# The expert stage of a two-layer transformer block: gathered rows turned by transposing DMAs instead of by TensorE

## The chip, the cores and the metric

The kernel runs on one core of a Trainium2 chip. The metric is the device time of one execution in microseconds; the median over the runs is quoted. A profile of one execution gives every instruction of the engines: TensorE (PE, and PEld for its weight loads), VectorE (DVE), ScalarE (ACT), GpSimd (POOL), SyncE (SP, which here only issues DMAs and waits).

## The reference

Two layers run over x of 16 x 100 tokens by 512. Only the end of the second layer, a mixture of 32 experts, is touched by the change:

```python
logits = x @ gate_weight.T                     # 1600 tokens, 32 experts
topv, topi = top_k(softmax(logits), 8)         # then scaled, cut at TAU, renormalised -> combine
def expert_step(acc, xs):
    w_gu, w_d, c_e = xs
    gu = x @ w_gu.T                            # 512 -> 2 x 192
    g, u = split(gu, 2)
    h = silu(g) * u
    acc = acc + h @ w_d.T * c_e[:, None]       # 192 -> 512
```

The result is added to x. Before it come an attention with latent keys, a feed-forward layer with ternary weights and a second, causal attention, each on a layer norm of x.

## The kernel before

Only the rows that an expert is really chosen for are computed. The stage `route` sorts the (token, expert) pairs into 131 tiles of up to 128 rows, each tile of one expert, and writes the row numbers to `core.sources`. The normed rows lie in HBM in `xtab`: for each token 512 columns of 4 bytes, which hold 1024 half-precision numbers (the 512 numbers as a high and a low half), and behind them 32 weights, one per expert.

The stage `experts` then goes through the tiles. The engines run their own programs, and semaphores order them:

- POOL (line 2686 on) gathers tile i + 8 by an indirect DMA into one of NX = 8 slots of `xg`, and scatters the finished rows of a tile with an add into one of NACC = 2 sums in HBM (`acc`). Scatter i waits for scatter i - 2 to have landed, and a gather into a slot waits until that slot's rows were turned.
- TensorE (line 2714 on) turns the gathered rows (`turn_x`): eight transposes of 128 x 128 into the bank `x_ps`, since the contraction must lie along the partitions. `up` makes 12 matmuls with 384 columns into `g_ps` (high and low halves of both operands, without low times low), `turn_h` turns h by three transposes into `h_ps`, and `downs` makes five matmuls with 512 columns into `d_ps`.
- VectorE copies `x_ps` to `xT` (`copy_x`, two buffers), multiplies (`product`), and makes the low half of h (`low`).
- ScalarE applies the silu (`silu`), makes the high half of h (`high`), copies `h_ps` to `hT` (`copy_h`) and scales the finished rows by the expert's weight (`weigh`).
- SP loads the weights of the next experts into a ring of four (line 2345 on), once the tiles of an older expert are done.

TensorE's order in the step of tile i is: `downs(i - 2)`, `turn_x(i + 1)`, the first half of `up(i)`, `turn_h(i - 1)`, the second half of `up(i)`. ScalarE's is: `weigh(i - 2)`, `copy_h(i - 1)`, `silu(i)`, `high(i)`. VectorE's is: `copy_x(i + 1)`, `product(i)`, `low(i)`. At the end the two sums in HBM are loaded, added and stored.

Of the kernel before, what the change touches and what calls it, by code (L numbers as in the profile page):

```python
# [19 lines left out]
ACT = mybir.ActivationFunctionType  # L20
# [5 lines left out]
P = 128  # L26
# [2299 lines left out]
TABLE = -(-TILES // GROUP) * GROUP  # L2326
FAR = 32768.0
ROUND = 1.5 * 2.0 ** 23
NX, NACC, NO = 8, 2, 6


class ExpertWeights:
# [289 lines left out]
def experts(core, t, ew, out):  # L2622

    nc = core.nc
    x_in = Slots(core, "slots_in", NX, per=16)
    x_turned, x_copied = Steps(core, "x2_turned"), Steps(core, "x2_copied")
    gu, gated, made = Steps(core, "gu2_sum"), Steps(core, "silu2"), Steps(core, "h2")
    h_hi, h_lo = Steps(core, "h2_hi"), Steps(core, "h2_lo")
    h_turned, h_copied = Steps(core, "h2_turned"), Steps(core, "h2_copied")
# [5 lines left out]
    back, summed, stored = Slots(core, "acc_back", PARTS, per=16 * NACC), core.sem("acc_summed"), core.sem("stored")  # L2635
    with ExitStack() as ctx:
        xg = core.xg
        xT = core.sb(ctx, "xT", [P, 2, 2 * KT, P], F16)
        sg = core.sb(ctx, "sg2", [P, 2, INTER], F32)
        hf = core.sb(ctx, "hf2", [P, 2, INTER], F32)  # L2640
        hc = core.sb(ctx, "hc2", [P, 2, 2, INTER], F16)
# [1 line left out]
        rows = core.sb(ctx, "rows2", [P, NO, DIM], F32)  # L2643
        total = [core.accT[:, :, :].rearrange("p k n -> p (k n)")]
        total += [core.sb(ctx, f"end_rows{k}", [P, FLAT], F32) for k in range(1, NACC)]
        x_ps = core.banks(ctx, "x2_ps", 2, F32)
        g_ps = core.banks(ctx, "g2_ps", 2)
        h_ps = core.banks(ctx, "h2_ps", 2, F32)
        d_ps = core.banks(ctx, "d2_ps", 2)
# [1 line left out]
        def half(bank, n):  # L2651
            return bank[:, 0:n * P // 2].bitcast(F16).rearrange("p (k s) -> p k s", k=n)
# [7 lines left out]
        with nc.Block() as block:  # L2660
# [24 lines left out]
            @block.gpsimd  # L2685
            def _(pool):
                def gather(i):
                    if i >= NX:
                        pool.wait_ge(x_turned.sem, x_turned.after(i - NX))
                    nc.gpsimd.indirect_dma_start(  # L2690
                        out=xg[:, i % NX, :], out_offset=None, in_=core.xtab[:, :],
                        in_offset=bass.IndirectOffsetOnAxis(ap=core.sources[:, i:i + 1], axis=0),
                        bounds_check=TOK - 1, oob_is_err=False).then_inc(x_in[i % NX].sem, 16)

                def scatter(i):
                    pool.wait_ge(weighed.sem, weighed.after(i))
                    if i >= NACC:
                        o = i - NACC
                        pool.wait_ge(put[o % NO].sem, put[o % NO].after(o // NO))
                    nc.gpsimd.indirect_dma_start(  # L2700
                        out=core.acc[i % NACC][:, :],
                        out_offset=bass.IndirectOffsetOnAxis(ap=core.sources[:, i:i + 1], axis=0),
                        in_=rows[:, i % NO, :], in_offset=None, bounds_check=TOK - 1, oob_is_err=False,
                        compute_op=ALU.add).then_inc(put[i % NO].sem, 16)

                for i in range(NX):
                    gather(i)
                for i in range(TILES):
                    scatter(i)
                    if i + NX < TILES:  # L2710
                        gather(i + NX)

            @block.tensor
            def _(pe):
                place = {}

                def turn_x(i):
                    pe.wait_ge(x_in[i % NX].sem, x_in[i % NX].after(i // NX))
                    if i >= 2:
                        pe.wait_ge(x_copied.sem, x_copied.after(i - 2))  # L2720
                    parts = xg[:, i % NX, 0:DIM].bitcast(F16)
                    for k in range(2 * KT):
                        last = nc.tensor.transpose(half(x_ps[i % 2], 2 * KT)[:, k, :], parts[:, k * P:(k + 1) * P],  # L2723
                                                   core.ident_h[:, :])
                    last.then_inc(x_turned.sem, 1)

                def ring(i, col, n, parts=P):
                    return ew.ring[0:parts, bass.ds(place[i][0] + col, n)]

# [13 lines left out]

                def up(i, terms):
                    if terms[0] == TERMS[0]:
                        pe.wait_ge(x_copied.sem, x_copied.after(i))
                        if i >= 2:
                            pe.wait_ge(made.sem, made.after(i - 2))
                        pe.wait_ge(w_ready, place[i][1])
                    for k, w, a in terms:  # L2750
                        last = nc.tensor.matmul(g_ps[i % 2][:, 0:2 * INTER], xT[:, i % 2, a * KT + k, :],  # L2751
                                                ring(i, (2 * k + w) * 2 * INTER, 2 * INTER),
                                                start=((k, w, a) == TERMS[0]), stop=((k, w, a) == TERMS[-1]))
                    if terms[-1] == TERMS[-1]:
                        last.then_inc(gu.sem, 1)
# [20 lines left out]

                load_place(0)
                check_place(0)
                turn_x(0)
                for i in range(TILES + 2):  # L2780
                    if i >= 2:
                        downs(i - 2)
                    if i + 1 < TILES:
                        turn_x(i + 1)
                    if i < TILES:
                        up(i, TERMS[0:6])
                    if 1 <= i < TILES + 1:
                        turn_h(i - 1)
                    if i < TILES:
                        up(i, TERMS[6:9])  # L2790
                    if i + 1 < TILES:
                        if (i + 1) % GROUP == 0:
                            load_place(i + 1)
                        check_place(i + 1)
                    if i < TILES:
                        up(i, TERMS[9:12])

            @block.scalar
            def _(act):
                col = {}  # L2800

                def silu(i):
                    act.wait_ge(gu.sem, gu.after(i))
                    if i >= 2:
                        act.wait_ge(made.sem, made.after(i - 2))
                    nc.scalar.activation(sg[:, i % 2, :], g_ps[i % 2][:, 0:INTER], ACT.Silu, scale=1.0 / W2  # L2806
                                         ).then_inc(gated.sem, 1)

                def high(i):
                    act.wait_ge(made.sem, made.after(i))  # L2810
                    if i >= 2:
                        act.wait_ge(h_turned.sem, h_turned.after(i - 2))
                    nc.scalar.activation(hc[:, i % 2, 0, :], hf[:, i % 2, :], ACT.Copy).then_inc(h_hi.sem, 1)  # L2813

                def copy_h(i):
                    act.wait_ge(h_turned.sem, h_turned.after(i))
                    if i >= 2:
                        act.wait_ge(down.sem, down.after(i - 2))
                    nc.scalar.activation(hT[:, i % 2], half(h_ps[i % 2], 3), ACT.Copy).then_inc(h_copied.sem, 1)  # L2819

                def weigh(i):
                    if i % GROUP == 0:
                        _, regs = nc.values_load_multi_w_load_instructions(
                            core.tile_tab[0:1, i // GROUP, 2, :], engines=[mybir.EngineType.Activation],
                            min_val=0, max_val=DIM + NEXP - 1,
                            skip_runtime_bounds_check_because="made from an expert's number, at most NEXP - 1")
                        for g in range(GROUP):
                            col[i + g] = regs[g]
                    act.wait_ge(down.sem, down.after(i))
                    if i >= NO:  # L2830
                        act.wait_ge(put[i % NO].sem, put[i % NO].after(i // NO - 1))
                    scale = xg[:, i % NX, bass.ds(col[i], 1)]
                    nc.scalar.activation(rows[:, i % NO, :], d_ps[i % 2][:, :], ACT.Copy, scale=scale  # L2833
                                         ).then_inc(weighed.sem, 1)

                for i in range(TILES + 2):
                    if i >= 2:
                        weigh(i - 2)
                    if 1 <= i < TILES + 1:
                        copy_h(i - 1)  # L2840
                    if i < TILES:
                        silu(i)
                        high(i)

            @block.vector
            def _(dve):
                def copy_x(i):
                    dve.wait_ge(x_turned.sem, x_turned.after(i))
                    if i >= 2:
                        dve.wait_ge(gu.sem, gu.after(i - 2))  # L2850
                    nc.vector.tensor_copy(xT[:, i % 2], half(x_ps[i % 2], 2 * KT)).then_inc(x_copied.sem, 1)  # L2851

                def product(i):
                    dve.wait_ge(gated.sem, gated.after(i))
# [8 lines left out]
                    nc.vector.tensor_tensor(hc[:, i % 2, 1, :], hf[:, i % 2, :], hc[:, i % 2, 0, :], ALU.subtract  # L2863
                                            ).then_inc(h_lo.sem, 1)

                copy_x(0)
                for i in range(TILES):
                    if i + 1 < TILES:
                        copy_x(i + 1)
                    product(i)  # L2870
                    low(i)
                for k in range(PARTS):
                    dve.wait_ge(back[k].sem, back[k].after(0))
                    nc.vector.tensor_tensor(total[0][:, piece(k)], total[0][:, piece(k)], total[1][:, piece(k)],  # L2874
# [110 lines left out]
```

## Time and profile before

| what | value |
|---|---|
| time, three runs | 1844.2, 1845.92, 1846.16 us; median 1845.92 |
| span of the profiled execution, first to last instruction | 1842.9 us |
| busy in the span: PE, DVE, ACT, POOL | 87%, 65%, 56%, 33% |
| mean granted TensorE clock over the span | 0.931 |
| expert stage: first gather, last `d_ps` group, last scatter begin at | 1323.81, 1812.15, 1814.98 us |

The profile states no time of its own for its execution beside the span; the median of the runs is 3.0 us above the span. In the profile an instruction stands with its engine, its line, and the tiles that it writes and reads (`out<-in`). A granted clock of 1.00 means 2.4 GHz, 0.50 means 1.2 GHz. The DMA share is the mean busy share of the core's 16 DMA engines. q1 is the queue of DMAs that SP issues, q10 that of ScalarE's, q0 that of POOL's.

### The profile page before, as it was taken

How to read it: one execution, taken by the hardware profiler on the slowest of the kernel's cores; microseconds unless marked ns; L12 is line 12 of the kernel's file. 1: busy time of each engine (PE TensorE's matmuls, PEld its weight loads, DVE VectorE, ACT ScalarE, POOL GpSimd, SP SyncE). 2: the span in 40 equal slices, each digit the busy share in tenths (PEclk: the TensorE clock that was granted, in tenths of full speed). 3: DMA queues.
4: the chain of work that ended last, by engine and by line, in shares of the span. 5: the costliest groups of instructions: out<-in, count | busy, mean ns of one | idle time of the engine just before them, and what ended most of it. 6: DMA issues, size and time to landing. Idle time of an engine off the chain costs nothing. (4 is left out here: it accounts for less than half of the span.)

```text
span 1842.9 us, 35610 instructions
## 1 busy us (share of the span) xinstructions
PE 1606.8 (87%) x11911; PEld 998.5 (54%) x11911; DVE 1192.0 (65%) x2678; ACT 1036.1 (56%) x2563; POOL 611.1 (33%) x481
## 2 busy tenths in 40 slices
PE   4788999999999979989997777784599999999993
PEld 3655656656656545555554454553466666666661
DVE  4866797787787779688796777757633333333332
ACT  3447746746747627566574777743655555455451
POOL 4614304304304300000000222212167777777662
PEclk9789999999999989999998998776599999999996
DMA  8820120220120249787786001104356656556536
GB/s 271 285 84 9 55 75 9 62 68 10 65 65 10 69 157 333 239 280 241 227 260 227 12 2 37 36 29 114 78 108 140 150 136 140 137 129 136 131 74 225
DMA packets 143332, 226.57 MB, mean 123 GB/s; under 512 B 37857, under 2 KB 93409, under 8 KB 143032
## 3 DMA queue, kind: packets, MB, share of 16 engines
q1 hardware_dynamic: 107160, 195.90, 33.6%
q0 software_dynamic: 29344, 21.29, 7.1%
q10 hardware_dynamic: 6656, 7.11, 1.1%
q8 instruction: 105, 1.72, 0.4%
q14 instruction: 67, 0.55, 0.1%
HBM read 175.00 MB, written 98.80 MB: 149 GB/s over the span
## 5 line engine op out<-in xcount | busy, mean ns | idle before, releaser
L2751 PE MATMUL g_ps<-ring,xT 128*128 x1572 | 300.8, 327 | 1.1 <-issue 1.1
L1051 POOL TENSOR_TENSOR pr<-pr,sm 128x1444 f32<-128x1444 f32 (+1 forms) x64 | 137.3, 2145 | 385.9 <-DVE sm L1087 385.9
L2700 POOL DMA_INDIRECT acc<-rows,slot_sources x131 | 207.8, 1586 | 107.2 <-issue 78.7
L2857 DVE SCALAR_TENSOR_TENSOR hf<-sg,g_ps 128x192 f32<-128x192 f32 x131 | 46.4, 354 | 238.5 <-ACT sg L2806 206.3
L2751 PEld LDWEIGHTS g_ps<-ring,xT 128*128 128x128 f16 x1572 | 142.8, 98 | 71.9 <-issue 5.5
L2690 POOL DMA_INDIRECT xg<-xtab,slot_sources x131 | 138.0, 1054 | 81.3 <-issue 79.5
L2773 PE MATMUL d_ps<-ring,hT 128*128 x655 | 162.8, 379 | 1.6 <-ACT hT L2819 1.1
L1081 DVE TENSOR_REDUCE sm<-s_banks 128x2 f32<-128x722 f32 (+2 forms) x128 | 97.5, 762 | 67.3 <-PE s_banks L819 64.8
L973 ACT ACTIVATE pr<-s_banks,sm 128x361 f32<-128x361 f32 (+1 forms) x208 | 115.3, 563 | 30.7 <-DVE sm L1081 29.2
L876 PE MATMUL o_bank<-cT,N_hi 128*128 128x400 f16 x512 | 129.7, 335 | 0.0
L819 PE MATMUL s_banks<-kvp,qp 128*128 128x361 f16 (+1 forms) x624 | 116.9, 318 | 10.8 <-ACT pr L973 6.1
L2098 POOL MEMSET zero_row<- 128x544 f32 x1 | 0.6, 557 | 377.5 <-POOLq L1338 377.5
L2819 ACT ACTIVATE hT<-h_ps 128x384 f16<-128x384 f16 x131 | 64.3, 491 | 101.8 <-PE h_ps L2764 99.3
L849 PE MATMUL o_bank<-probsT,kvp 128*128 128x384 f16 (+5 forms) x576 | 108.2, 333 | 1.1 <-DVE probsT L1092 1.1
L1230 ACT ACTIVATE split_o<-split_f 128x512 f16<-128x512 f32 (+1 forms) x192 | 87.9, 513 | 20.6 <-DMA split_f<-in_down 12.1
L2773 PEld LDWEIGHTS d_ps<-ring,hT 128*128 128x128 f16 x655 | 63.7, 97 | 65.6 <-issue 3.4
L2102 POOL TENSOR_TENSOR pr<-pr,sm 100x1600 f32<-100x1600 f32 x16 | 45.8, 2864 | 157.5 <-DVE sm L2173 157.5
L2833 ACT ACTIVATE rows<-d_ps,xg 128x512 f32<-128x512 f32 x131 | 90.0, 687 | 13.4 <-issue 2.2
L2851 DVE COPY xT<-x_ps 128x1024 f16<-128x1024 f16 x131 | 90.6, 692 | 10.1 <-issue 6.2
L1376 PE MATMUL gate_ps<-hT_hi,wt 128*128 128x400 f16 x256 | 86.8, 339 | 11.0 <-DVE hf L1506 9.2
L1396 PE MATMUL down_ps<-hid,wt 128*128 128x400 f16 x512 | 94.5, 345 | 0.7 <-DVE hid L1511 0.7
L2723 PEld LDWEIGHTS x_ps<-ident_h,xg 128*128 128x128 f16 x1048 | 70.0, 99 | 37.5 <-DMA xg<-xtab,slot_sources 7.1
(322 smaller groups left out, 3848.1 us busy)
## 6 DMA issues: line engine op xcount, KB each, us to landing
split_f<-in_gu SPq DMA_DIRECT2D x64, 384.0 KB, 4.5
split_gu<-split_o SPq DMA_DIRECT2D x64, 384.0 KB, 3.1
ring<-split_gu SPq DMA_DIRECT2D x32, 768.0 KB
head<-in_head SPq DMA_DIRECT2D x16, 864.0 KB
tern_w<-in_tern SPq DMA_DIRECT2D x48, 256.0 KB
split_f<-in_down SPq DMA_DIRECT2D x32, 384.0 KB, 4.2
split_d<-split_o SPq DMA_DIRECT2D x32, 384.0 KB, 3.8
ring<-split_d SPq DMA_DIRECT2D x32, 256.0 KB
```

Source lines behind the costliest of these rows:

```text
L819: last = nc.tensor.matmul(sbank[0:n, i, 0:KEYS], qp[:, a, bi, at:at + n], kvp[:, bi % 2, k].rearrange("p j d -> p (j d)")[:, 0:KEYS], star ...
L849: last = nc.tensor.matmul(ob[1][:, 0:width(s)], kvp[0:KEYT[u], bi % 2, k, u, :], pT[s % 2][0:KEYT[u], a, u, 0:width(s)], start=(j == 0), s ...
L876: op = nc.tensor.matmul(ob[m % 2][:, 0:CH], w[:, h, f], cT[:, a, :, h * SEQ:(h + 1) * SEQ], start=(t == 0), stop=(t == len(terms) - 1))
L973: nc.scalar.activation(pr[0:n, s % 3, i, :], sbank[0:n, i, 0:KEYS], ACT.Exp, bias=small[0:n, s % 3, 0, i:i + 1], accum_out=small[0:n, s % ...
L1051: nc.gpsimd.tensor_tensor(pr[:, s % 3, 0:n], pr[:, s % 3, 0:n], small[:, s % 3, 2, 0:n].unsqueeze(2).to_broadcast([P, n, KEYS]), ALU.mult) ...
L1081: nc.vector.tensor_reduce(small[0:n, s % 3, 0, first:last], sbank[0:n, first:last, 0:KEYS], AX, ALU.max, negate=True).then_inc(peak.sem, 1)
L1396: last = nc.tensor.matmul(d_ps[m % 2][:, 0:CH], core.wt[:, 2 * KT * HT // 4 + k, m * P:(m + 1) * P], hh[:, a, k, :], start=(k == 0 and a = ...
L2690: nc.gpsimd.indirect_dma_start(out=xg[:, i % NX, :], out_offset=None, in_=core.xtab[:, :], in_offset=bass.IndirectOffsetOnAxis(ap=core.sou ...
L2700: nc.gpsimd.indirect_dma_start(out=core.acc[i % NACC][:, :], out_offset=bass.IndirectOffsetOnAxis(ap=core.sources[:, i:i + 1], axis=0), in ...
L2751: last = nc.tensor.matmul(g_ps[i % 2][:, 0:2 * INTER], xT[:, i % 2, a * KT + k, :], ring(i, (2 * k + w) * 2 * INTER, 2 * INTER), start=((k ...
L2773: last = nc.tensor.matmul(d_ps[i % 2][:, :], hT[0:parts, i % 2, pair, :], ring(i, D + col * DIM, DIM, parts), start=(n == 0), stop=(n == 4))
L2851: nc.vector.tensor_copy(xT[:, i % 2], half(x_ps[i % 2], 2 * KT)).then_inc(x_copied.sem, 1)
```

## The change

The eight transposes of TensorE and VectorE's copy of their result go. In their place ScalarE issues one transposing DMA a tile, from `xg` (128 rows of 1024 half-precision numbers) straight into `xT`, which has NT = 4 buffers with a semaphore each. It is issued three tiles ahead, between `weigh(i - 2)` and `silu(i)`; it waits until the gather has landed and until the matmuls that read the buffer before are done. TensorE's `up(i)` waits for that DMA, and so does POOL's gather into the slot. VectorE takes `copy_h` over from ScalarE. The two PSUM banks `x_ps` are no longer used.

```diff
-NX, NACC, NO = 8, 2, 6
+NX, NACC, NO, NT = 8, 2, 6, 4
...
-    x_turned, x_copied = Steps(core, "x2_turned"), Steps(core, "x2_copied")
+    x_turned = Slots(core, "x2_turned", NT, per=16)
...
-        xT = core.sb(ctx, "xT", [P, 2, 2 * KT, P], F16)
+        xT = core.sb(ctx, "xT", [P, NT, 2 * KT, P], F16)
...
                 def gather(i):
                     if i >= NX:
-                        pool.wait_ge(x_turned.sem, x_turned.after(i - NX))
+                        o = i - NX
+                        pool.wait_ge(x_turned[o % NT].sem, x_turned[o % NT].after(o // NT))
...
-                def turn_x(i):
-                    pe.wait_ge(x_in[i % NX].sem, x_in[i % NX].after(i // NX))
-                    if i >= 2:
-                        pe.wait_ge(x_copied.sem, x_copied.after(i - 2))
-                    parts = xg[:, i % NX, 0:DIM].bitcast(F16)
-                    for k in range(2 * KT):
-                        last = nc.tensor.transpose(half(x_ps[i % 2], 2 * KT)[:, k, :], parts[:, k * P:(k + 1) * P],
-                                                   core.ident_h[:, :])
-                    last.then_inc(x_turned.sem, 1)
...
                     if terms[0] == TERMS[0]:
-                        pe.wait_ge(x_copied.sem, x_copied.after(i))
+                        pe.wait_ge(x_turned[i % NT].sem, x_turned[i % NT].after(i // NT))
...
-                turn_x(0)
                 for i in range(TILES + 2):
                     if i >= 2:
                         downs(i - 2)
-                    if i + 1 < TILES:
-                        turn_x(i + 1)
...
-                def copy_h(i):
-                    act.wait_ge(h_turned.sem, h_turned.after(i))
-                    if i >= 2:
-                        act.wait_ge(down.sem, down.after(i - 2))
-                    nc.scalar.activation(hT[:, i % 2], half(h_ps[i % 2], 3), ACT.Copy).then_inc(h_copied.sem, 1)
+                def turn_x(i):
+                    act.wait_ge(x_in[i % NX].sem, x_in[i % NX].after(i // NX))
+                    if i >= NT:
+                        act.wait_ge(gu.sem, gu.after(i - NT))
+                    nc.scalar.dma_start_transpose(xT[:, i % NT], xg[:, i % NX, 0:DIM].bitcast(F16)
+                                                  ).then_inc(x_turned[i % NT].sem, 16)
...
+                for i in range(NT - 1):
+                    turn_x(i)
                 for i in range(TILES + 2):
                     if i >= 2:
                         weigh(i - 2)
-                    if 1 <= i < TILES + 1:
-                        copy_h(i - 1)
+                    if i + NT - 1 < TILES:
+                        turn_x(i + NT - 1)
                     if i < TILES:
                         silu(i)
                         high(i)
...
-                def copy_x(i):
-                    dve.wait_ge(x_turned.sem, x_turned.after(i))
+                def copy_h(i):
+                    dve.wait_ge(h_turned.sem, h_turned.after(i))
                     if i >= 2:
-                        dve.wait_ge(gu.sem, gu.after(i - 2))
-                    nc.vector.tensor_copy(xT[:, i % 2], half(x_ps[i % 2], 2 * KT)).then_inc(x_copied.sem, 1)
+                        dve.wait_ge(down.sem, down.after(i - 2))
+                    nc.vector.tensor_copy(hT[:, i % 2], half(h_ps[i % 2], 3)).then_inc(h_copied.sem, 1)
...
-                copy_x(0)
-                for i in range(TILES):
-                    if i + 1 < TILES:
-                        copy_x(i + 1)
-                    product(i)
-                    low(i)
+                for i in range(TILES + 1):
+                    if i >= 1:
+                        copy_h(i - 1)
+                    if i < TILES:
+                        product(i)
+                        low(i)
```

## Rows read from the trace of the kernel before

**Rows 1.** View by windows: us, busy us of each engine, PEclk, DMA share, GB/s.

```profile
1372.00:1422.00 50.00, 49.96 (x382) 30.87 (x380) 18.86 (x41) 25.16 (x55) 35.98 (x28) 1.00 0.62 135
...
1722.00:1772.00 50.00, 49.59 (x382) 30.78 (x381) 19.51 (x42) 25.72 (x55) 36.13 (x28) 1.00 0.51 120
```

**Rows 2.** The view by lines, 1350 to 1840 us, forms kept apart.

```profile
L2700 POOL DMA_INDIRECT acc<-rows,slot_sources x128 | 203.0, 1586 | 100.4 <-issue 78.4 <-ACT rows L2833 19.2 <-DMA acc<-rows,slot_sources 2.8
...
L2690 POOL DMA_INDIRECT xg<-xtab,slot_sources x121 | 127.5, 1054 | 36.9 <-issue 35.1 <-DMA acc<-rows,slot_sources 1.8
L2833 ACT ACTIVATE rows<-d_ps,xg 128x512 f32<-128x512 f32 x128 | 87.9, 687 | 13.0 <-issue 2.2 <-PE d_ps L2773 0.8
L2851 DVE COPY xT<-x_ps 128x1024 f16<-128x1024 f16 x125 | 86.5, 692 | 2.9 <-PE x_ps L2723 0.2
...
L2819 ACT ACTIVATE hT<-h_ps 128x384 f16<-128x384 f16 x127 | 62.4, 491 | 98.8 <-PE h_ps L2764 96.3 <-issue 2.4
```

**Rows 3.** The timeline of one tile, start us, us, engine.

```profile
1569.65 0.49 ACT L2819 ACTIVATE hT<-h_ps 128x384 f16<-128x384 f16 x1 [0.52 <-PE h_ps L2764]
...
1570.42 1.24 PE L2773 MATMUL d_ps<-ring,hT 128*128 x5
1570.62 0.33 ACT L2806 ACTIVATE sg<-g_ps 128x192 f32<-128x192 f32 x1 [0.48 <-PE g_ps L2751]
...
1571.77 0.36 DVE L2863 TENSOR_TENSOR hc<-hf,hc 128x192 f16<-128x192 f32 x1 [0.43 <-ACT hc L2813]
1571.88 0.69 ACT L2833 ACTIVATE rows<-d_ps,xg 128x512 f32<-128x512 f32 x1
...
1572.76 0.32 PEld L2764 LDWEIGHTS h_ps<-ident_h,hc 128*128 128x128 f16 x3
```

**Rows 4.** The timeline of TensorE, the last tiles.

```profile
1802.54 1.24 PE L2773 MATMUL d_ps<-ring,hT 128*128 x5
...
1806.18 1.24 PE L2773 MATMUL d_ps<-ring,hT 128*128 x5
...
1809.38 1.24 PE L2773 MATMUL d_ps<-ring,hT 128*128 x5
```

**Rows 5.** The timeline of POOL beside a load of weights.

```profile
1566.80 1.59 POOL L2700 DMA_INDIRECT acc<-rows,slot_sources  x1 [1.50 <-DMA acc<-rows,slot_sources]
1568.70 1.05 POOL L2690 DMA_INDIRECT xg<-xtab,slot_sources  x1 [0.30 <-issue]
1570.06 1.59 POOL L2700 DMA_INDIRECT acc<-rows,slot_sources  x1 [0.31 <-issue]
...
1573.37 1.59 POOL L2700 DMA_INDIRECT acc<-rows,slot_sources  x1 [0.32 <-issue]
```

**Rows 6.** DMA queues of 1350 to 1800, 16 to 114, 1815.5 to 1823 us: packets, MB, share.

```profile
q1 hardware_dynamic: 33152, 38.55, 30.1%
q0 software_dynamic: 27299, 19.18, 26.3%
...
q10 hardware_dynamic: 6656, 7.11, 21.1%
...
q1 hardware_dynamic: 463, 2.66, 93.5%
```

**Rows 7.** DMA issues: ns min/median/max of three lines, then one's landing in us.

```profile
L475 ACTq DMA_DIRECT2D lat_parts<-lat_parts_sb x16: 520/521/581, 18.1 to 111.6; - x16
...
L473 ACTq DMA_DIRECT2D kv_parts<-kv_parts_sb x16: 321/327/352, 17.7 to 111.2; - x16
...
L2352 SPq DMA_DIRECT2D ring<-split_d x32: 626/632/1705, 1277.6 to 1753.4; - x32
...
ternary<-tern_o SPq DMA_DIRECT2D x48, 128.0 KB, 1.7
```

**Rows 8.** The timeline of POOL and TensorE at the stage's start.

```profile
1323.81 1.28 POOL L2690 DMA_INDIRECT xg<-xtab,slot_sources  x1 [41.68 <-issue]
...
1327.61 1.04 PE L2723 MATMUL x_ps<-ident_h,xg 128*128 128x128 f16 x8 [6.06 <-DMA xg<-xtab,slot_sources]
```

More of the change, by code:

```diff
@@ L2645, in experts @@
         total += [core.sb(ctx, f"end_rows{k}", [P, FLAT], F32) for k in range(1, NACC)]
-        x_ps = core.banks(ctx, "x2_ps", 2, F32)
         g_ps = core.banks(ctx, "g2_ps", 2)
@@ L2750, in up @@
                     for k, w, a in terms:
-                        last = nc.tensor.matmul(g_ps[i % 2][:, 0:2 * INTER], xT[:, i % 2, a * KT + k, :],
+                        last = nc.tensor.matmul(g_ps[i % 2][:, 0:2 * INTER], xT[:, i % NT, a * KT + k, :],
                                                 ring(i, (2 * k + w) * 2 * INTER, 2 * INTER),
```

## The prediction

> **What bounds the kernel now.** I first read the windows of the expert stage, from the profile's start of the tile loop to its end, to see which engine has no gaps. Of eight windows of 50 us TensorE is busy 49.96 us in the first and 49.59 us in the last, at a granted clock of 1.00, which is the 2.4 GHz level [rows 1]. So the stage runs at TensorE's pace, and what is taken from TensorE there shortens the kernel until the next engine is full. The view by lines gives the price of each operation [rows 2], the timeline of one tile gives the order in which the engines hand work to each other [rows 3], and the timeline of the last tiles gives something rare: a tile of the same loop without the turning of x. From one start of the `d_ps` group to the next it is 3.64 us with the eight transposes (1802.54 to 1806.18) and 3.20 us without (1806.18 to 1809.38) [rows 4]. The timeline of POOL and the DMA views then give the two resources that are next [rows 5, 6].
>
> **What the change removes.** On TensorE: eight transposes a tile. By [rows 4] that is worth 3.64 - 3.20 = 0.44 us a tile, over 130 tile steps 57 us, and TensorE's own limit is then 3.20 us a tile. On VectorE: a copy of 692 ns a tile, replaced by the copy of h, 384 columns of 1024. Its price is between 692 x 384/1024 = 260 ns and ScalarE's 491 ns for the same tile [rows 2]. I take the middle, 0.38 us. ScalarE's copy now ends 0.28 us before the `d_ps` group that reads it (1570.14 against 1570.42) [rows 3], and VectorE's, which waits on the same `h_ps`, would not end later, so it costs nothing at either end. On ScalarE those 491 ns go. One cover gets thinner: the low half of h is ready at 1572.13, and TensorE loads it at 1572.76 [rows 3]; without the transposes ahead of it TensorE comes 0.44 us sooner, and 0.19 us are left. Whatever delays the silu by more than that is paid in full.
>
> **The scatter and gather engine is next.** POOL needs per tile 1.586 us for a scatter and 1.054 us for a gather [rows 2], with at least 0.31 and 0.30 us between them [rows 5]: 3.25 us, seen where it runs without waiting (1566.80 to 1570.06 in 3.26 us). It has 3.64 now. So of the 0.44 us at most 0.39 can be had: 3.25 us a tile instead of 3.20. The other thing POOL loses is its slack. Scatter number i waits for scatter i - 2 to land. At 1566.80 it waited 1.50 us instead of 0.31, during the transfer of an expert's weights [rows 5]; at 3.64 us a tile such a wait was made up in the next tiles, at 3.25 it is not. The ring holds four of the 32 experts at the start, so the stage loads 28, one in 131/28 = 4.7 tiles. If each cost this wait once, that were 1.19/4.7 = 0.25 us a tile; if none, 0. I take two of three, 0.17 us, because the time a scatter has to land falls by 2 x 0.39 = 0.78 us and the DMA engines get more to do. This gives 3.42 us a tile.
>
> **What the transposing DMA costs the DMA engines.** No row of before shows one. It moves 128 rows of 1024 half words, 256 KB. If a piece is one row of one block of 128 columns, 256 B, these are 1024 pieces, 64 for each of the 16 engines. The stage now uses 30.1 + 26.3 = 56.4% of the engines [rows 6], 2.05 us a tile. ScalarE's own queue moved 6656 packets in the first stage at 21.1% of 16 engines x 98 us, 49.7 ns for a mean of 1068 B; the large packets of the end took 93.5% x 16 x 7.5 us/463 = 242 ns for 5745 B, 42 ns for 1000 B [rows 6]. The first price is then 45 ns for bytes and 5 ns for the packet, and a piece of 256 B costs 11 + 5 = 16 ns: 64 pieces, 1.0 us. The weight loads in the stage cost 65 ns for 1163 B, 16 ns more than their bytes; by them a piece costs 27 ns, the transfer 1.7 us. At the full 49.7 ns it is 3.2 us. The bounds are 1.0 and 3.2 us. I take 1.0, since the row of ScalarE's queue is the nearest: same queue, SBUF as source, small pieces. The engines then have 3.05 us of work in 3.42, which is full but fits. Latency is covered: three transfers are ahead of the tile that is computed, 3 x 3.42 = 10 us, and a plain transfer of 128 KB lands in 1.7 us [rows 7].
>
> **What it costs ScalarE.** From the start of a silu to the end of the weighing after it 1.95 us pass (1570.62 to 1572.57) [rows 3]; then the new issue stands in ScalarE's queue, and behind it the next silu, for which VectorE's product, the turning of h and a later `d_ps` group wait. ScalarE's loop is thus 1.95 us + issue, and an issue up to 3.25 - 1.95 = 1.3 us is hidden by the TensorE work of the same tile; above that each microsecond lengthens each tile. Issues of plain DMAs on this queue took 327 ns (128 rows) and 521 ns (256 pieces), and one of SP's in the stage 632 ns, at worst 1705 ns [rows 7]. If the time grows by 194 ns for each further 128 pieces, 1024 pieces take 0.327 + 7 x 0.194 = 1.69 us. Bounds 0.33 and 1.69. I take 0.6, since SP's issue of several pieces a row does not grow so. The issue also waits for a gather three tiles ahead. The gather of tile j follows scatter j - 8. In tile step j - 6 the weighing ends 2.15 us after the `d_ps` group began, the scatter starts 0.80 us later (1572.57, 1573.37) [rows 3, 5], and with 1.59 + 0.30 + 1.05 us the gather is written out at 5.9 us. The first gather of the stage landed within 2.5 us after that (1325.09 to 1327.61) [rows 8], so it is there at 8.4 us, and ScalarE asks for it three steps later, at 3 x 3.25 + 2.15 = 11.9 us. The wait costs nothing while gathers land within 6 us; if POOL falls behind by more than 3.5 us, ScalarE holds the silu for it.
>
> **The start.** The first tile is turned by a transfer that lands in 1.7 us or more [rows 7], in place of eight transposes of 1.04 us [rows 8] and a copy of 0.69: between 0 and, with the issue and the weight loads beside it, some 3 us later. I take +1 us. Nothing after the last tile changes.
>
> **The sum.** 130 x (3.64 - 3.42) = 29 us, less 1: 28 us below the profiled execution's span of 1842.9. The median of the runs is 3.0 us above that span, and I keep that difference: 1845.9 - 28 = 1818 us. What such a measurement can tell from no change is 0.2%, 3.7 us.
>
> **Rivals.**
> - **The DMA engines become the bound (slower).** Place: the 16 engines in the stage, which weights, gathers, scatters and transposes share. For it: 56% are used already, the stage's own packets cost 65 ns, and the wait at 1566.80 shows that weight loads hold small transfers up. Against: the price by bytes. A tile then takes 2.05 us + the transfer; it decides from 1.59 us up, just below the 1.7 of the weight loads' row. At 1.7 it is 3.75 us, +14 us and the start, 1861; at 3.2 it is 5.25 us, +209, 2056. The Trainium skill (DMA: Bandwidth & Descriptors, Issuing engines are not separate DMA queues) has the rule behind it: whoever issues, the same 16 engines do the work. The wait at 1566.80 agrees.
> - **Blocks one after another (much slower).** If the eight blocks of 128 x 128 don't overlap and each pays a landing as 128 KB does, 1.7 us, a tile takes 13.6 us: +1295 us, 3141; at half of that 6.8 us, +410, 2257. Nothing in the profile speaks for it, and nothing excludes it, since no such transfer is in it. The Trainium skill (VectorE: DVE Perf Modes, The three transpose paths) gives 1309 ns for such a block by DMA and 390 ns by TensorE, which would be an estimated 8 x 1.309 = 10.5 us a tile; no run here shows it yet.
> - **ScalarE's issue fills what TensorE gave up (no change).** With 1.69 us a tile takes 1.95 + 1.69 = 3.64 us, what it takes now: 1847 with the start. It decides above 1.3 us.
> - **All waits of scatters kept.** With one wait for each weight load 3.50 us a tile, 1828; with 1.5 of them 3.63, 1845. This is the upper end of my own case, whose lower end is 3.25 us: 1796.
>
> **Chances and range.** My case 0.52 (own range 1796 to 1845), ScalarE's issue 0.12, DMA engines 0.31, one after another 0.05. Faster by over 0.2%: nearly all of my case and a little of ScalarE's, 0.52. Within 0.2%: 0.02 + 0.07 = 0.09. Slower: 0.39. The range runs from 1796 to 2000; below it 0.04, above it the upper quarter of the DMA case and the serial one, 0.13.
>
> **What would show it.** Right: no `x_ps` group; `d_ps` groups 3.3 to 3.5 us apart; POOL's scatters with 0.31 us before most of them; ScalarE's queue below 1.3 us an issue; its transfers landing in under 6 us. Wrong: matmuls of `up` waiting for `xT` (the transfers are too slow), silu waiting behind the issue with TensorE idle (ScalarE), a DMA share near 1.0 over the whole stage, or a granted clock below 1.00 because TensorE waits.

## The result, and the profile after

The changed kernel takes 1897.18 us (median of four runs, 1884.31 to 1912.8) against 1846.04 us for the kernel before. It is slower by 51 us, where 28 us less were forecast. The ratio is 1.0268, with an interval of 1.0227 to 1.031; it leaves out the run of 1912.8 us, a slow one, over 1.5% above the fastest. The profiled execution is the fastest of the four (1884.31 us, span 1882.7 us), so the sums below explain 40 us, and the other runs are 10 to 28 us worse.

The DMA queues of the changed kernel from 1350 to 1800 us, with packets, MB and share of 16 engines, answer to [rows 6]:

```profile
q10 hardware_dynamic: 118202, 29.36, 48.8%
q1 hardware_dynamic: 32716, 38.17, 33.4%
q0 software_dynamic: 25035, 17.81, 23.1%
```

q10 is new here: the transposing DMAs. A packet of theirs costs 48.8% x 16 x 450 us/118202 = 29.7 ns, about the 27 ns that the weight loads' row gave and not the 16 ns that I took. The three shares add to 105%. A share above 100% says that records of one engine overlap, so it shows pressure, not how much room is left.

Two of the same windows as in [rows 1]: TensorE was busy 49.96 and 49.59 us there.

```profile
1372.00:1422.00 50.00, 44.98 (x267) 23.55 (x266) 13.93 (x39) 17.98 (x40) 33.81 (x26) 0.98 1.14 198
...
1722.00:1772.00 50.00, 40.91 (x229) 20.90 (x228) 12.21 (x34) 14.93 (x34) 31.77 (x24) 0.93 1.06 167
```

TensorE has gaps now, and the granted clock falls to 0.93, an average over stretches at 2.4 and at 1.2 GHz. The last weight load is issued from 1791.61 to 1795.95. The timeline of TensorE behind it begins with such a gap: TensorE waits 3.54 us for a turned tile, and then six matmuls of `up` take 2.10 us instead of 1.14.

```profile
1805.23 2.10 PE L2741 MATMUL g_ps<-ring,xT 128*128 x6 [3.54 <-DMA xT<-xg]
...
1811.30 1.14 PE L2741 MATMUL g_ps<-ring,xT 128*128 x6
...
1813.41 1.24 PE L2763 MATMUL d_ps<-ring,hT 128*128 x5
...
1816.61 1.24 PE L2763 MATMUL d_ps<-ring,hT 128*128 x5
...
1819.81 1.24 PE L2763 MATMUL d_ps<-ring,hT 128*128 x5
...
1823.00 1.24 PE L2763 MATMUL d_ps<-ring,hT 128*128 x5
...
1826.09 0.66 PE L2741 MATMUL g_ps<-ring,xT 128*128 x3 [0.21 <-issue]
1826.58 1.24 PE L2763 MATMUL d_ps<-ring,hT 128*128 x5
```

The view by windows of the slow stretch gives a granted clock of 0.51, the 1.2 GHz level (columns as in [rows 1]):

```profile
1805.30:1811.20 5.90, 5.90 (x20) 2.70 (x21) 1.78 (x5) 2.07 (x5) 4.36 (x5) 0.51 1.08 172
```

From 1813.41 on three tiles take 3.20 us each, as [rows 4] promised, with transposing DMAs, gathers and scatters running. The fourth takes 3.58 us (1823.00 to 1826.58), with a gap before the last three matmuls of `up`.

Beside a weight load it looks like this (timeline of all engines, start us, duration us, engine):

```profile
1561.13 0.55 SPq L2350 DMA_DIRECT2D ring<-split_gu  x1
...
1562.40 1.73 ACTq L2806 DMA_TRANSPOSE xT<-xg  x1
...
1563.18 1.24 PE L2763 MATMUL d_ps<-ring,hT 128*128 x5
...
1565.08 0.61 SPq L2356 DMA_DIRECT2D ring<-split_d  x1
...
1566.90 3.03 ACTq L2806 DMA_TRANSPOSE xT<-xg  x1
...
1567.67 1.24 PE L2763 MATMUL d_ps<-ring,hT 128*128 x5
...
1570.04 0.33 ACT L2793 ACTIVATE sg<-g_ps 128x192 f32<-128x192 f32 x1 [4.12 <-issue]
...
1571.60 0.34 PE L2754 MATMUL h_ps<-ident_h,hc 128*128 128x128 f16 x3 [1.71 <-DVE hc L2853]
...
1572.82 1.24 PE L2763 MATMUL d_ps<-ring,hT 128*128 x5
```

Read it from the load on. SP issues the six DMAs from 1561.13 to 1565.69. ScalarE's transposing issue before the next silu begins at 1566.90, 4.50 us after the one before, and lasts 3.03 us. The silu behind it starts at 1570.04, although its sum was there soon after the `d_ps` group began at 1567.67. TensorE then waits 1.71 us for the low half of h. The two tile steps take 4.49 and 5.15 us instead of 3.20. The issue itself, over the whole kernel (ns min/median/max):

```profile
L2806 ACTq DMA_TRANSPOSE xT<-xg x131: 1247/1365/3553, 1330.6 to 1837.6; - x131
```

The same loss is in the chain that ended last. Its shares of the span by line begin as follows, before the change and then after it:

```profile
by line: PE g_ps L2751 13.7%; PE d_ps L2773 7.6%; PE x_ps L2723 3.2%; PE h_ps L2764 1.2%; issue 0.6%; DMA accT<-acc 0.5%; DMA acc<-rows,slot_sources 0.4%; DMA xg<-xtab,slot_sources 0.2%; DVE accT L2874 0.1%; SPq L2677 0.1%; DVE hc L2863 0.0
by line: DMA xg<-xtab,slot_sources 6.1%; DMA acc<-rows,slot_sources 5.8%; PE g_ps L2741 3.6%; issue 3.2%; DMA xT<-xg 2.6%; PE d_ps L2763 2.1%; ACTq L2806 1.3%; POOL acc L2700 1.1%; POOL xg L2690 0.6%; DMA accT<-acc 0.5%; PE h_ps L2754 0.4%;
```

TensorE's matmuls led it before. Now gathers and scatters that have not landed lead it. A piece in order of time shows a gather that takes 9 us to land, the transposing issue behind it, and TensorE behind that.

```profile
1773.98 9.00 DMA xg<-xtab,slot_sources
1783.00 1.29 ACTq L2806
1786.30 1.00 PE g_ps L2741 x6
```

### The profile page after: what moved, and what is told of

Same layout as the page of the kernel before. It is cut to its first block and busy times, and to the rows that moved or that the text cites. A ratio compares the mean times of both kernels' runs of the same rounds, so it can differ in the third digit from the quotient of the medians.

```text
span 1882.7 us, 33364 instructions
## 1 busy us (share of the span) xinstructions
PE 1578.8 (84%) x10844; PEld 938.4 (50%) x10863; DVE 1147.5 (61%) x2678; ACT 966.2 (51%) x2432; POOL 611.4 (32%) x481
## 5 line engine op out<-in xcount | busy, mean ns | idle before, releaser
L2741 PE MATMUL g_ps<-ring,xT 128*128 x1572 | 316.0, 335 | 34.6 <-DMA xT<-xg 20.4
L2793 ACT ACTIVATE sg<-g_ps 128x192 f32<-128x192 f32 x131 | 43.2, 330 | 262.6 <-PE g_ps L2741 149.9
L2763 PE MATMUL d_ps<-ring,hT 128*128 x655 | 170.6, 393 | 0.5 <-DVE hT L2841 0.5
L973 ACT ACTIVATE pr<-s_banks,sm 128x361 f32<-128x361 f32 (+1 forms) x208 | 115.1, 562 | 30.7 <-DVE sm L1081 29.2
L2841 DVE COPY hT<-h_ps 128x384 f16<-128x384 f16 x131 | 46.9, 358 | 90.2 <-PE h_ps L2754 84.8
L1376 PE MATMUL up_ps<-hT_hi,wt 128*128 128x400 f16 x256 | 86.3, 337 | 0.0
```

Source lines behind the costliest of these rows:

```text
L973: nc.scalar.activation(pr[0:n, s % 3, i, :], sbank[0:n, i, 0:KEYS], ACT.Exp, bias=small[0:n, s % 3, 0, i:i + 1], accum_out=small[0:n, s % ...
L1376: last = nc.tensor.matmul(ps[:, 0:CH], weights(mt, k), a[:, k, bass.ds(c * CH, CH)], start=(k == 0 and a is core.hT_hi), stop=(k == KT - 1 ...
L2763: last = nc.tensor.matmul(d_ps[i % 2][:, :], hT[0:parts, i % 2, pair, :], ring(i, D + col * DIM, DIM, parts), start=(n == 0), stop=(n == 4))
```

## The experiments

**Without weight loads.** The 28 loads of the stage are left out, once in the kernel before and once in the changed one (experts 4 to 31 then use the weights of the first four, so the output is another one).

```diff
                 for e in range(NEXP):
-                    sp.wait_ge(ew.w_in[e % NB].sem, ew.w_in[e % NB].after(e // NB))
+                    if e < NB:
+                        sp.wait_ge(ew.w_in[e % NB].sem, ew.w_in[e % NB].after(e // NB))
                     sp.sem_inc(w_ready, 1)
-                    if e >= 2 and e - 2 + NB < NEXP:
-                        end = sp.value_load(core.end_tab[0:1, e - 2:e - 1], min_val=1, max_val=TILES + 1)
-                        sp.wait_ge(down.sem, end)
-                        ew.load(sp, e - 2 + NB)
```

> The kernel before, with the 28 weight loads of the expert stage left out (experts 4 to 31 use the weights of the four in the ring, so the output is another one). This is the control for the next run. Theory 1 (the DMA engines are full with the change, not before it): the loads were hidden, 1843 to 1847 us. Theory 2 (ScalarE's queue order) and theory 3 (gathers come too late) say the same here. A time more than 10 us lower would mean that weight loads already cost something before the change.

> The changed kernel with the same 28 weight loads left out (output changed in the same way). Theory 1: the DMA share falls from about 1.0 to about 0.75, every tile takes 3.20 to 3.28 us as the last tiles of the changed kernel do, and the time is 1790 to 1805 us. Theory 2 (each issue stands before a silu in ScalarE's queue, whatever else the DMA engines do): an issue keeps its 1.25 us or more and the time stays above 1840 us. If the transposing transfers set the pace by themselves: no change, 1885 us.

Measured, with one run each: 1847.57 us for the kernel before, so its loads were hidden, and 1807.8 us for the changed one, 37 us faster than the kernel before on the same chip (1844.99). The change does what it is for, as long as no weight loads run beside it. The first and the last `d_ps` matmul of the changed kernel, with loads and without (view of the tile `d_ps`, ns min/median/max, first and last start):

```profile
L2763 PE MATMUL d_ps<-ring,hT x655: 379/379/634, 1341.3 to 1852.9; 128*128 x164 
```

```profile
L2760 PE MATMUL d_ps<-ring,hT x655: 379/379/388, 1339.1 to 1776.3; 128*128 x164 
```

Over 130 tile steps, less 0.9 us for the last group itself, that is 3.93 us a tile with loads and 3.36 without. The difference, 74 us, is 2.7 us for each of 28 loads. The maximum of 634 ns, against 379, belongs to matmuls at the lower clock.

Without loads nearly all of what is left above 3.20 us lies in every fourth step (from one start of a `d_ps` group to the next). All 32 of those take 3.58 us or more (median 3.62) and make 18.7 of the 20.9 us, while the others have a median of 3.20. In the kernel before all four positions have a median of 3.64. The view of waits, 1350 to 1800 us, has the gap at `up`, first in the kernel before and then in the changed one without loads:

```profile
PEld g_ps L2751 <- issue: 2.9, 7, 0.8
```

```profile
PEld g_ps L2738 <- issue: 24.0, 36, 1.3
```

There, between the ninth and the tenth matmul of `up`, TensorE's program reads where the weights of the next four tiles lie (`load_place`). That the reading itself costs the 0.4 us is not shown.

**ScalarE's order and the lead of the gathers.** Two ways to make the waits harmless without changing the work.

```diff
-                    if i + NT - 1 < TILES:
-                        turn_x(i + NT - 1)
                     if i < TILES:
                         silu(i)
                         high(i)
+                    if i + NT - 1 < TILES:
+                        turn_x(i + NT - 1)
```

```diff
-NX, NACC, NO, NT = 8, 2, 6, 4
+NX, NACC, NO, NT = 11, 2, 6, 4
```

> The changed kernel with ScalarE's transposing DMA issued behind silu and the high half of h instead of before them; same work, same lead. Theory 1 (DMA engines full): the same within the scatter of the changed kernel, 1880 to 1905 us, and a DMA share still near 1.0. Theory 2 (the engines have room, but a slow issue or a late gather holds the silu behind it): 1810 to 1835 us.

> The changed kernel with 11 slots for gathered rows instead of 8, so that a gather starts three tiles earlier. Theory 3 (the change needs gathers three tiles earlier than before, and ScalarE waits for them although the DMA engines have room): 1810 to 1840 us. Theory 1 (DMA engines full): the same as with 8 slots, 1880 to 1905 us, since more lead gives no more transfers per microsecond. Theory 2: the same as with 8 slots.

Measured: 1916.88 us (ratio to before 1.0409, 1.038 to 1.0438) and 1927.0 us (1.0441, 1.0393 to 1.049). Neither gives anything back; both are worse than the changed kernel. Theories 2 (the order in ScalarE's queue) and 3 (the lead of the gathers) fall as causes by themselves. With the issue last, TensorE waits elsewhere, 57.1 us for turned tiles (view of waits, 1350 to 1800 us) against 6.9 us in the changed kernel, and scatters land no sooner: a median of 7.0 us, and 6.5 us with 11 slots, against 6.9. Why the two are worse by 20 and 30 us was not followed further; with 11 slots POOL waited 108.0 us for scatters to land (same view), against 40.8 us with 8.

**One part alone: VectorE copies h.** The kernel before with `copy_h` on VectorE, TensorE still turning x.

```diff
 # ScalarE
-                    if 1 <= i < TILES + 1:
-                        copy_h(i - 1)
...
 # VectorE
+                    if i >= 1:
+                        copy_h(i - 1)
```

> The kernel before with one part of the change alone: VectorE copies the turned rows of h instead of ScalarE, TensorE still turns x. Theory 1 (DMA engines full) and the prediction: no cost, 1843 to 1847 us. Rival: VectorE, which then makes four operations a tile in order, delays a hand-over and part of the loss lies here: 1855 us or more.

Measured: 1847.22 us, ratio 1.001 (0.9996 to 1.0025). This part is free, at 358 ns a copy.

**Transfers that nobody waits for.** The kernel of the last run with an extra DMA of 256 KB a tile, issued by ScalarE before the silu, from `hT_hi` to spare buffers, of which TensorE uses nothing. It is made three ways: transposing, as a plain copy in rows of 2 KB, and as a plain copy in 1024 pieces of 256 B.

```diff
+                def turn_spare(i):
+                    if i >= 2:
+                        act.wait_ge(spare_in[i % 2].sem, spare_in[i % 2].after(i // 2 - 1))
+                    nc.scalar.dma_start_transpose(spare[:, i % 2], core.hT_hi[:, 0, 0:2 * KT * P]
+                                                  ).then_inc(spare_in[i % 2].sem, 16)
```

> The kernel before with VectorE's copy of h, and beside it one transposing DMA of 256 KB a tile that nobody uses: from a buffer that is not written in this stage into two spare buffers, issued by ScalarE at the place of the change. TensorE still turns x and waits for none of these transfers. Theory 1 (the transfers fill the DMA engines and hold up gathers, scatters and weights): the DMA share rises to about 1.0 and a tile takes about 3.9 us, 1870 to 1895 us. Rival (the loss comes from waiting for the turned rows themselves, their latency or lead): 1843 to 1850 us, since no engine but ScalarE's next issue waits for them.

> As the run with unused transposing transfers, but each is a plain copy of the same 256 KB between the same two buffers, in rows of 2 KB (128 pieces instead of 1024). If the bytes fill the engines: a tile slows as with the transposes, 1890 us or more. If the number of small pieces or the transposing does it: 8 pieces an engine by some 85 ns each are 0.7 us, 2.05 + 0.7 = 2.75 us a tile, 1845 to 1855 us.

> The same plain copy cut into 1024 pieces of 256 B, as many as the transposing transfer has. If the number of small pieces fills the engines, whether transposed or not: 1880 to 1925 us and some 23 to 30 ns a piece. If it is the transposing itself that holds other transfers up: 1845 to 1860 us, with pieces that cost no more than the 16 ns of the prediction.

Measured: 1920.43 us transposing (ratio 1.0412, 1.0391 to 1.0432), 1859.03 us in rows (1.0072, 1.0046 to 1.0097), 1853.87 us in pieces (1.0055, 1.0036 to 1.0074). The queue rows of 1350 to 1800 us, transposing and then in pieces:

```profile
q10 hardware_dynamic: 113994, 28.31, 46.2%
```

```profile
q10 hardware_dynamic: 121684, 30.68, 33.4%
```

A transposed piece costs 46.2% x 7200 us/113994 = 29.2 ns, a plain one 19.8 ns. So neither the bytes nor the number of pieces make the loss. Transposing does: 74 us against 9 in pieces and 15 in rows, each against the kernel before on the same chip.

In the transposing run the silu waited 84.8 us behind the issue, which itself waits for a spare buffer. This is a confound (in pieces it was 42.3 us). The next run uses six buffers, in a tensor that the stage does not use otherwise.

```diff
+    NS = 6
...
-                    if i >= 2:
-                        act.wait_ge(spare_in[i % 2].sem, spare_in[i % 2].after(i // 2 - 1))
+                    if i >= NS:
+                        act.wait_ge(spare_in[i % NS].sem, spare_in[i % NS].after(i // NS - 1))
```

> The run with unused transposing transfers again, but into six buffers in turn instead of two, so that ScalarE waits only for the landing of the transfer six tiles back, which it had to wait for two tiles back in that run. If the transfers hold up everything else by filling the DMA engines (theory 1): still 1880 us or more. If that run was slow because ScalarE itself stood waiting for late landings with a silu behind it: 1850 to 1865 us, like the plain copies, and the DMA engines' fill is only a condition for the late landings.

Measured: 1935.96 us (1.0501, 1.0467 to 1.0535), not less, although the silu's wait for these buffers falls to 19.6 us. That wait was not the cause. In its place TensorE and POOL wait for landings (view of waits, 1350 to 1800 us: total, times, longest):

```profile
POOL acc L2704 <- DMA acc<-rows,slot_sources: 123.9, 31, 8.2
PEld x_ps L2727 <- DMA xg<-xtab,slot_sources: 59.0, 25, 6.8
...
PE x_ps L2727 <- DMA xg<-xtab,slot_sources: 47.0, 20, 6.3
```

The transfers of other queues come late: the scatters' 2.8 us of waits in [rows 2] have become 123.9, and TensorE stands still for gathered rows, not for ScalarE, whose longer issue (up to 6.9 us here) would otherwise be a rival cause: only 6.1 us of its waits are for the low half of h. Plain copies raise the scatters' waits too, to 46.9 us in pieces, but behind the start of the stage no gather is among the longest pieces of the chain that ended last there. Plain copies with six buffers were not run.

**Fewer blocks by DMA.** The first `BY_DMA` of the eight blocks are turned by DMA and the rest by TensorE as before the change, with VectorE's copy for those.

```diff
+                    for k in range(BY_DMA, 2 * KT):
+                        last = nc.tensor.transpose(half(x_ps[i % 2], 2 * KT)[:, k, :], parts[:, k * P:(k + 1) * P],
+                                                   core.ident_h[:, :])
...
-                    nc.scalar.dma_start_transpose(xT[:, i % NT], xg[:, i % NX, 0:DIM].bitcast(F16)
+                    nc.scalar.dma_start_transpose(xT[:, i % NT, 0:BY_DMA],
+                                                  xg[:, i % NX, 0:DIM].bitcast(F16)[:, 0:BY_DMA * P]
```

> The changed kernel with only the first four of the eight blocks of 128 columns turned by DMA (128 KB a tile); TensorE turns the other four as before the change, and VectorE copies them. Theory 1: DMA work per tile falls to 2.05 + 0.8 to 0.96 = 2.9 to 3.0 us, TensorE needs 3.20 + 0.22 = 3.42 us, so TensorE is the bound again: 1815 to 1832 us, faster than both. Rival (weight loads and transposing transfers disturb each other however small the transfers are, every load costs its wait): half of the loss stays, 1855 to 1875 us.

> The kernel that turns half of the blocks by DMA, with the 28 weight loads of the stage left out (experts 4 to 31 use the weights of the four in the ring, so the output is another one). Theory 1: without the loads its transfers fit, TensorE sets 3.42 us a tile, 1815 to 1822 us, 25 to 30 below the same kernel with loads. Rival (half by DMA has a cost of its own, as its copy and its order on VectorE): 1840 us or more.

> The same with two of eight blocks by DMA (64 KB a tile). Theory 1: DMA work 2.05 + 0.4 to 0.48 = 2.5 us, TensorE 3.53 us a tile: 1828 to 1838 us. Rival (each load costs its wait): 1845 to 1860 us.

> Two of eight blocks by DMA up to tile 115 and all eight from tile 116 on, where the trace of before shows no weight load any more. Theory 1: the gain of the quarter version, 13 us, and 15 x (3.53 - 3.20) = 5 us more: 1825 to 1832 us, faster than both kernels. Rival (the transposing transfer costs more than TensorE's transposes also beside gathers and scatters alone): 1835 us or more.

Measured: half 1847.04 us (1.0016, 1.0 to 1.0033), half without loads 1823.88 us, a quarter 1833.24 us (0.9928, 0.9908 to 0.9948), a quarter and then the whole 1833.88 us (0.994, 0.9923 to 0.9958). The quarter beats both kernels. The half lies 15 us above its forecast range, and without loads (one run) it misses the forecast for that by 2 us only, so here too the loads take the gain. The last version gave nothing beyond the quarter; the forecast 5 us are within its interval. The issue costs nearly the same whatever it moves. ScalarE's row for half and for a quarter:

```profile
L2824 ACTq DMA_TRANSPOSE xT<-xg x131: 1204/1222/2683, 1327.9 to 1787.5; - x131
```

```profile
L2824 ACTq DMA_TRANSPOSE xT<-xg x131: 1182/1186/2280, 1328.4 to 1796.7; - x131
```

**Mean work or bursts.** The same bytes, but a load's six DMAs not issued at once: first each after the landing of the one before, then only in two steps.

```diff
 # in load(), after the first DMA of 768 KB; in the other version after each of the six
+        if e >= NB:
+            sp.wait_ge(sem, 96 * (e // NB) + 16)
```

> The changed kernel with weight loads that are spread in time: SP issues each of the six DMAs of an expert's load only when the one before has landed. The same bytes and pieces. If the mean work of the DMA engines is the bound (theory 1, as stated): 1880 to 1905 us, no gain. If the bursts of a load are what delays landings (the engines have room on average): 1830 to 1870 us.

> Two of eight blocks by DMA, with the same spread loads. TensorE needs 3.53 us a tile, 1828 to 1832 us at best. If bursts cost the quarter version something: 1828 to 1831 us; if not: 1833 us, the same as without spreading.

Measured: 2084.51 us (1.127, 1.1233 to 1.1307) and 2020.08 us (1.0936, 1.0908 to 1.0965). Inconclusive: a load now takes some 21 us (first DMAs of two loads issued at 1501.46 and 1522.07), longer than the time between two, and TensorE waits for weights (view of waits of the first of them):

```profile
PE g_ps L2749 <- SPq L2674: 141.0, 17, 14.1
```

> The changed kernel with each weight load in two steps: SP issues the first DMA (768 KB) and the other five (576 KB) only when it has landed. In the version with six steps a load took some 21 us and TensorE waited for weights, which hid the answer; two steps should take 9 to 11 us, less than the 4.7 tiles between two loads. If the mean work of the DMA engines is the bound: 1880 to 1915 us. If the bursts do it: 1840 to 1870 us. If TensorE waits for weights again, the run says nothing.

> Two of eight blocks by DMA, with loads in two steps. The DMA engines have room here, so it is where shorter bursts could show: 1827 to 1831 us if they cost something, 1833 us if not.

> Four of eight blocks by DMA, with weight loads in two steps. If the depth of a load's burst is what the half version paid for (1847 us instead of the 1817 that TensorE's 3.42 us a tile would give): 1818 to 1832 us, faster than both kernels and at least as fast as the quarter version. If it is the mean work of the DMA engines: 1847 us, unchanged.

Measured: the changed kernel with loads in two steps 1857.62 us (1.0063, 1.0028 to 1.0098), a quarter 1833.7 us (0.9929, 0.9905 to 0.9954), half 1830.93 us (0.9933, 0.9916 to 0.9951). One wait of SP in each load takes 40 of the 51 us away. The queues of the first, 1350 to 1800 us, and its `d_ps` row:

```profile
q10 hardware_dynamic: 127413, 31.64, 52.3%
q1 hardware_dynamic: 33152, 38.55, 31.6%
q0 software_dynamic: 26947, 19.23, 24.2%
```

```profile
L2765 PE MATMUL d_ps<-ring,hT x655: 379/379/634, 1342.4 to 1823.4; 128*128 x164 
```

A transposed piece still costs 29.6 ns and the shares add to 108%, more than in the changed kernel, and yet a tile takes 3.69 us instead of 3.93. So the engines were not full on average. Theory 1 falls in the form in which it was stated. How much of a load is issued at once, beside transposing transfers, makes 40 us of the loss. It does not make all that the loads cost: 1857.62 us are still 50 us above the 1807.8 us without loads, and no run here takes that part further.

## Why the prediction was wrong

**What bounds the kernel: right. What the change removes: right for three tiles of four.** Removing the transposes is worth 3.64 - 3.20 = 0.44 us in these: tiles without a load beside them take 3.20 us. Every fourth keeps 3.58 us or more, which is some 12 us less gain. The prediction read TensorE's limit from one tile step, and that step was not a fourth one. VectorE's copy is free (0.358 us, 0.38 taken).

**POOL next: right as a floor, wrong in the waits.** Scatters run 3.25 us apart in the quiet tiles (1817.05, 1820.30, 1823.55). TensorE's four steps there average 3.29 us, so that POOL's floor bound it is not shown. The term that failed is "I take two of three, 0.17 us": one wait of 1.19 us for two of three loads, 22 us in all. A load cost 2.7 us on average, 74 us in all. The row I sized it by was a scatter's wait in a kernel without transposing transfers.

With it failed the limit that the prediction set itself: ScalarE's wait for a gather "costs nothing while gathers land within 6 us", with a landing taken from the first gather of the stage, 2.5 us. The view of the gathers' line, and then of the scatters', in the changed kernel:

```profile
DMA to landing us min/median/max: 2.5/6.1/9.9
DMA to landing us min/median/max: 2.7/6.9/11.5
```

Half of the gathers take longer than that limit, which was reckoned for tiles of 3.25 us. In the kernel before without loads the medians are 3.3 and 3.2 us. ScalarE's in-order queue and the two-deep scatter pass the delay on to TensorE, which has 0.19 us of cover. TensorE's largest wait is the one for the low half of h, which stands behind ScalarE's silu (view of waits, 1350 to 1800 us):

```profile
PE h_ps L2754 <- DVE hc L2853: 41.0, 32, 3.3
```

**The price on the DMA engines: mis-sized.** 1.0 us was taken; 64 packets at 29.7 ns are 1.9 us. The plain pieces at 19.8 ns, 1.27 us, show that the sum by bytes was low by a fifth for plain copies, and that transposing adds half as much again in the same place. It is no fixed price, since a packet's time grows with what runs beside it: 26.0 ns without loads (47.2% x 7200 us/130811), 25.7 ns with loads in the half version (23.9%, 66914 packets) and 19.5 ns in the quarter version (9.6%, 35433). The Trainium skill (Advanced Engine Details and Errata, X-Bar Transpose (TRN2)) states that transposing DMAs are as fast as regular ones on this chip. In the full mixture that does not hold: 29.2 against 19.8 ns, measured on the same 256 KB.

**ScalarE's issue: mis-sized, and hidden as computed.** 0.6 us was taken, 1.25 us is the least. At 1.25 us it just fits below the 1.3 us from which it was to cost something, which the 3.20 us tiles show. What was not foreseen is that it stretches: its median over the whole kernel is 1.37 us, and beside a load it lasts 3.0 us and more, in front of a silu.

**The sum for the profiled execution.** The tile steps took 3.66 us on average before and would take 3.20: -60 us. Above that floor the kernel without loads stays at 3.36: +20 us, nearly all of it in the fourth steps, where 6 us were forecast for POOL's floor. Loads: +74 us, against 22. The first `d_ps` group starts 4.7 us later, 3.05 us of that already at the first gather (1326.86 against 1323.81), ahead of any new instruction; the rest is close to the 1 us taken. Together +39 us; the spans differ by 39.8.

**The rivals.** The DMA rival had the right place and nearly the right number: 2.05 + 1.9 = 3.95 us a tile against 3.93 measured, 1887 us. But its mechanism, engines whose mean work is the bound, was refuted by the loads in two steps. A forecast can come close for a reason that doesn't hold. The serial rival is out: eight blocks and all else fit in tiles of 3.20 us, and the first transfer of the stage landed in 3.77 us (chain that ended last):

```profile
1330.59 3.77 DMA xT<-xg
```

So the 1309 ns that the Trainium skill (VectorE: DVE Perf Modes, The three transpose paths) gives for a block do not add up over eight blocks here. The issue as a bound of every tile is out too, since tiles of 3.20 us contain it. The Trainium skill (DMA: Bandwidth & Descriptors, Issuing engines are not separate DMA queues) states that DMAs run on the same 16 engines whoever issues them. The run with unused transposes agrees: ScalarE's transfers, which nobody needs, delay POOL's.

**What stays open.** That transposing transfers beside weight loads make gathers and scatters land late, and that a load issued in two steps does so less, is shown; by what in the DMA engines a transposed piece does so, while a plain one of the same size hardly does, is not. Nor is it shown what the 50 us are that the loads still cost in two steps, or why every fourth step keeps 3.58 us.

## What to carry to other kernels

Before work is moved to DMA, don't ask only whether the mean DMA time fits: look for the deepest burst of other transfers, and for what stands in order behind a landing or an issue beside it; the price is paid there. Here one wait on a load's first transfer split the burst. Look also at more than one step of a loop before its floor is taken from a row: here every fourth was longer. If a full move overshoots, a part of it may be the optimum: a quarter of the blocks by DMA, or half of them with loads in two steps, gave 0.993 of the time before.

## What the runs showed of the hardware that was not expected

- The issue of a transposing DMA from SBUF to SBUF holds ScalarE's queue for about 1.2 us whether it moves 64, 128 or 256 KB (1182, 1204, 1247 ns at least); plain copies of the same 256 KB took 472 ns in rows and 602 ns in 1024 pieces.
- A transposed 256 B piece took 29 ns of an engine beside weight loads when all blocks went by DMA, 19.5 ns when a quarter did, and 22.8 ns in the quiet end of the stage (32.2% x 16 x 28 us/6336 packets, 1822 to 1850 us); a plain piece took 19.8 ns beside loads.
- More lead made it worse: 11 gather slots instead of 8 cost some 30 us, with transposing transfers in the queue.
